# Bilinear block of a four-block fp32 network: the whole stacked image made by identity matmuls, in pieces between the convolution chunks, with no transfers

## Chip, cores and metric

The program runs on one core of one Trainium2 chip. The metric is the device time of one execution in microseconds; the times shown are medians of several executions. TensorE (PE; PEld is its weight load), VectorE (DVE), ScalarE (ACT), GpSimd (POOL) and SyncE (SP) run side by side and meet at semaphores. SBUF is the on-chip memory of 128 partitions, PSUM holds what TensorE writes, in eight banks (`ps[0]` to `ps[7]`) of 512 fp32 columns.

## The reference

Four residual blocks, each on the group-normalised image; x has 4 images of 32 channels of 64x64 pixels, in fp32. The change is in the second one.

```python
x = x + _L0_conv_ref(_gn(x), ...)   # dynamic convolution of 3x3 taps
x = x + _L1_conv_ref(_gn(x), L1_conv_weights, L1_conv_tap_offsets)   # the bilinear block
x = x + _L2_conv_ref(_gn(x), ...)   # four gated experts of two convolutions
x = x + _L3_conv_ref(_gn(x), ...)   # mixed weights, two convolutions
# _L1_conv_ref: nine taps with fractional offsets
ry = xp[:, :, y0i, :] * (1.0 - fy) + xp[:, :, y1i, :] * fy
tap = ry[:, :, :, x0i] * (1.0 - fx) + ry[:, :, :, x1i] * fx
out = jnp.einsum('kbiyx,oik->boyx', jnp.stack(taps, 0), weights)
```

With offsets from 0 to 3 every tap is a mix of pixels in a 4x4 window, so the block is one 4x4 convolution, whose weights (`WE`) are mixed once from the nine taps and their offsets.

## The kernel before

The image lies in SBUF with 32 partitions for each of the 4 images (4 x 32 = 128). `IMG` is the padded, normalised image, 68 rows of 66 columns. For the bilinear block `SK` holds, for each image b, a stack of four copies of it: partitions 32g to 32g+31 hold image b shifted by g columns (g = 0 to 3). With that stack four columns of the window times 32 channels make a contraction over all 128 partitions, and only the four rows of the window are left to loop over.

`conv(k, ...)` (L773 to L779) computes chunk k of the output, 8 rows or 512 pixels of all images. It has 16 matmuls: for each window row y (4) and each image b (4) one of 128x32 weights against 512 columns, the four images beside each other in the four column strips of the array, into bank `k % 4`. An fp32 matmul stands in the trace as two records, so a chunk has 32. There are `NCH` = 8 chunks, on L810. Chunk k reads the rows 8k to 8k+10 of `SK`.

`SK` is filled in two ways. The first 27 rows are made in pieces (`PIECES`, L80): `copy_piece(n)` (L781 to L791) sends one piece's rows of `IMG` through an identity matrix (`REPL`), 16 matmuls of 32x32, for each image b and each shift g, into the banks 4 to 7 (one for each image). The matmuls use all 16 sub-arrays of 32x32 side by side. VectorE then copies the banks of images 0 and 1 to `SK` (L1026 to L1030), ScalarE those of images 2 and 3 (L643 to L647). A piece cannot begin before both have copied the piece before it (L784 to L786), since it writes the same banks. Pieces 0, 1 and 2 stand ahead of chunk 0, piece 3 behind it. The other 40 rows, in three parts (`STACK_DMA`, L81), are moved by DMA: `copy_rows` (L321 to L327) issues 16 transfers for a part. SyncE issues parts 0 and 1 (L418 to L422), then the weights of the next block, `W2A` and `W2B` (L423 to L426). ScalarE issues part 2 after chunk 2 (L648 to L651). Chunks 3, 5 and 7 wait for a part each (L806, L807).

The instructions of an engine run in the order in which they stand in its block. On VectorE `add2(k)` (L1034 to L1040) adds the bank of chunk k to X and takes the statistics of the result, and `x2_done` tells that the bank is free for chunk k+4. After chunk 7 the statistics are joined (`coefs(3)`), VectorE writes `CP`, and the first convolution of the next block (L840) can begin; before it TensorE runs small matmuls of that block (L826, L827) and seven matmuls with an unused result, `fill(7)` (L832). An `If` that handles offsets beyond the window (`far`) is not taken with these inputs.

```python
for k in range(NCH):                      # L802
    if k < 3: wait stack1_by_vector, stack1_by_scalar >= k + 2
    if k in (3, 5, 7): wait stack1_by_dma[k // 2 - 1] >= 16 * 16
    if k >= 4: wait x2_done >= k - 3
    conv(k, lambda y: WE[:, y, :], 4, conv1_done)
    if k == 0: copy_piece(3)
```

(the waits are shortened here.)

Of the kernel before, what the change touches and what calls it, by code (L numbers as in the profile page):

```python
# [35 lines left out]
B, C, H, W = 4, 32, 64, 64  # L36
# [6 lines left out]
PW = W + 2  # L43
# [32 lines left out]
Z_IMAGE = Z_WEIGHT + 3  # L76
Z_LATER = Z_IMAGE + 3


PIECES = ((0, 8), (8, 11), (11, 19), (19, 27))  # L80
STACK_DMA = ((27, 43), (43, 59), (59, 67))  # L81
IMG_V = 40
RELU_ROWS = ((8, 16), (16, 24), (24, 32), (32, 40), (6, 8), (40, 48), (48, 56), (56, H - 1))
N_RELU = len(RELU_ROWS)
# [8 lines left out]
def build(nc, x, w0, pw, cw, w1, w2a, w2b, w3a, w3b, par, out):  # L93
    ctx = ExitStack()
    with ctx:
# [12 lines left out]
        def sem(name):  # L108
            return ctx.enter_context(nc.semaphore(name))
# [3 lines left out]
        IMG, img_at, _ = sb("IMG", [P, PH * PW])  # L113
# [58 lines left out]
        SK = SKF[:, :].rearrange("p (b n) -> p b n", b=B)  # L172
# [28 lines left out]
        zeroed = sem("zeroed")  # L201
# [30 lines left out]
        image_by_vector = sem("image_by_vector")  # L232
        image_by_scalar = sem("image_by_scalar")
        stack_copied = sem("stack_copied")
        stack1_by_vector = sem("stack1_by_vector")
        stack1_by_scalar = sem("stack1_by_scalar")
        stack1_by_dma = [sem(f"stack1_by_dma{i}") for i in range(len(STACK_DMA))]
        conv1_done = sem("conv1_done")
        x2_done = sem("x2_done")
        norm2_done = sem("norm2_done")  # L240
# [76 lines left out]

        def copied_piece(b, r0, r1):
            return ps[4 + b][:, 0:(r1 - r0) * W].rearrange("p (r c) -> p r c", c=W)

        def copy_rows(queue, part):  # L321

            r0, r1 = STACK_DMA[part]
            a, n = r0 * PW, (r1 - r0 - 1) * PW + W
            for b in range(B):
                for g in range(4):
                    queue.dma_start(SK[32 * g:32 * g + 32, b, a:a + n], IMG[32 * b:32 * b + 32, a + g:a + g + n]).then_inc(stack1_by_dma[part], 16)  # L327

        def relu_px(i):
            r0, r1 = RELU_ROWS[i]  # L330
# [9 lines left out]
        def _(sp):  # L340
# [74 lines left out]
            stack_third(2 * STEPS, 0, REST * P)  # L415
            repeat_hi(0, REST * P, STEPS + 1)

            sp.wait_ge(zeroed, Z_IMAGE)  # L418
            sp.wait_ge(image_by_scalar, 1)
            copy_rows(sp, 0)  # L420
            sp.wait_ge(image_by_vector, 2)
            copy_rows(sp, 1)  # L422
            for g in range(4):  # L423
                p = slice(32 * g, 32 * g + 32)
                sp.dma_start(W2A[p, :, :].rearrange("p (x d) n -> p x (d n)", x=3), w2a.rearrange("(x c) d n -> c x (d n)", x=3)).then_inc(w_l2, 16)
# [1 line left out]
            for n in range(NCH):  # L427
                k = 2 * (n % 4) + 1 - n // 4
# [7 lines left out]
        def _(gp):  # L436
            n = [0]
# [128 lines left out]
            far = gp.value_load(FARN[0:1, 0:1], min_val=0, max_val=1)  # L566
            with gp.If(far > 0):
                gp.wait_ge(far_over, 1)
            gp.wait_ge(stack1_by_vector, len(PIECES))
            for m in (CP[:, :], HP[:, :, :], HQ[:, :, :]):  # L570
                gp.memset(m, 0.0).then_inc(zeroed, 1)
            rstd(3)
# [31 lines left out]
        def _(act):  # L604
# [24 lines left out]
            for pair in range(2):  # L629
                g = STEPS * TIT + 2 * pair  # L630
                n = min(2, NT - g)
# [6 lines left out]
                                      bias=NMR[p, 0:1], scale=RS[p, 0:1])  # L638

            act.wait_ge(coef_ready, 1)  # L640
            for r0, r1 in ((26, 42), (10, 26)):
                norm(rows(IMG, 1 + r0, r1 - r0), r0, r1).then_inc(image_by_scalar, 1)
            for n, (r0, r1) in enumerate(PIECES):  # L643
                act.wait_ge(stack_copied, n + 1)
                for b in (2, 3):
                    ins = act.activation(stack_piece(b, r0, r1), copied_piece(b, r0, r1), ACT.Copy)
                ins.then_inc(stack1_by_scalar, 1)  # L647
            act.wait_ge(zeroed, Z_IMAGE)  # L648
            act.wait_ge(image_by_vector, 2)
            act.wait_ge(conv1_done, 3)  # L650
            copy_rows(act, 2)  # L651

            act.wait_ge(coef_ready, 2)
            act.wait_ge(zeroed, Z_LATER)
            act.activation(U[:, :], X[:, :], ACT.Identity, bias=NMR[:, 0:1], scale=RS[:, 0:1]).then_inc(norm2_done, 1)
# [41 lines left out]
        def _(pe):  # L697
# [83 lines left out]
            def copy_piece(n):  # L781

                r0, r1 = PIECES[n]
                if n:  # L784
                    pe.wait_ge(stack1_by_vector, n)
                    pe.wait_ge(stack1_by_scalar, n)  # L786
                for b in range(B):
                    p = slice(32 * b, 32 * b + 32)
                    for g in range(4):
                        ins = pe.matmul(ps[4 + b][32 * g:32 * g + 32, 0:(r1 - r0) * W], REPL[p, 0, :], image_piece(b, r0, r1, g), start=True, stop=True)  # L790
                ins.then_inc(stack_copied, 1)  # L791
# [5 lines left out]
            pe.wait_ge(image_by_vector, 1)  # L797
            copy_piece(0)
            copy_piece(1)
            pe.wait_ge(image_by_scalar, 2)  # L800
            copy_piece(2)
            for k in range(NCH):  # L802
                if k < 3:
                    pe.wait_ge(stack1_by_vector, k + 2)
                    pe.wait_ge(stack1_by_scalar, k + 2)
                if k in (3, 5, 7):  # L806
                    pe.wait_ge(stack1_by_dma[k // 2 - 1], 16 * 16)  # L807
                if k >= 4:
                    pe.wait_ge(x2_done, k - 3)
                conv(k, lambda y: WE[:, y, :], 4, conv1_done)  # L810
                if k == 0:
                    copy_piece(3)

            pe.wait_ge(far_known, 1)
            far = pe.value_load(FARN[0:1, 0:1], min_val=0, max_val=1)
# [104 lines left out]
        def _(ve):  # L920
            n = [0]
# [101 lines left out]
            coefs(2)  # L1023
            norm(rows(IMG, 1, 10), 0, 10).then_inc(image_by_vector, 1)
            norm(rows(IMG, 43, H - 42), 42, H).then_inc(image_by_vector, 1)
            for i, (r0, r1) in enumerate(PIECES):  # L1026
                ve.wait_ge(stack_copied, i + 1)
                for b in (0, 1):
                    ins = ve.tensor_copy(stack_piece(b, r0, r1), copied_piece(b, r0, r1))
                ins.then_inc(stack1_by_vector, 1)  # L1030

            ve.wait_ge(far_known, 1)
            far = ve.value_load(FARN[0:1, 0:1], min_val=0, max_val=1)
            def add2(k):  # L1034

                ve.wait_ge(conv1_done, k + 1)
                xs = X[:, k * CH:(k + 1) * CH]
                ve.tensor_tensor(xs, ps[k % 4][:, :], xs, ALU.add).then_inc(x2_done, 1)
                ve.wait_ge(x2_done, k + 1)
                return ve.bn_stats(ST[:, k, :], xs)  # L1040

            for k in range(NCH - 1):
                add2(k)
            ve.wait_ge(image_by_scalar, 2)
            with ve.If(far > 0):
                ve.wait_ge(mix_ready, 1)
# [204 lines left out]
```

## Time and profile before

| | |
|---|---|
| median of 3 runs | 425.21 us (425.14 to 425.44) |
| the profiled execution | 425.92 us, of which the span is 424.1 us |
| mean granted TensorE clock over the span | 0.966 of full speed |
| TensorE matmuls busy | 382.5 us, 90% |
| VectorE busy | 276.4 us, 65% |
| ScalarE busy | 57.3 us, 14% |
| transfers SK<-IMG of SyncE | 32, 131.8 KB each, 2.6 us to landing |
| bilinear block on TensorE | from 276.06 to 313.57 us |

The span is the time from the first to the last instruction in the profile; times within it are counted from its start. "Releaser" is what ended an engine's wait. The clock of TensorE is given as a share of its full speed: 1.00 is 2.4 GHz, 0.50 is 1.2 GHz. The chain of work that ended last follows, from the last instruction back, what each step waited for, so that the sum of its steps is the time.

### The profile page before, as it was taken

To read this page: it belongs to the slowest core of one execution; us is meant where nothing else is said; L and a number is where in the kernel's file an instruction comes from. 1 tells how busy PE (TensorE), PEld (TensorE's weight loads), DVE (VectorE), ACT (ScalarE), POOL (GpSimd) and SP (SyncE) were. 2 spreads that over 40 slices of the span, in tenths; PEclk is the share of its full clock that TensorE was granted. 3 is DMA by queue.
4 is the path that set the end of the run, shared out by engine and by line. 5 is a ranking of instruction groups with operands and counts; after the bars stand their busy time and mean duration, and the time that the engine had idled before them with its cause. 6 is when DMAs were issued, how large, how long until landed. Compare 5 with 4: busy or idle time off the path is not lost.

```text
span 424.1 us, 8245 instructions
## 1 busy us (share of the span) xinstructions
PE 382.5 (90%) x3174; PEld 259.1 (61%) x3174; DVE 276.4 (65%) x486; ACT 57.3 (14%) x95; POOL 91.1 (21%) x220
## 2 busy tenths in 40 slices
PE   0799799999999999999999999479999979889892
PEld 0344588888888888888888888312247652157570
DVE  4981377777877888887787798844444077831155
ACT  0721000000000000000000000041013027552200
POOL 6687500688800000000000000105000037000000
PEclk9999799999999999999999999859999999899997
DMA  6276758055455545535613400068900000000023
GB/s 204 61 182 153 186 142 220 7 144 130 120 123 125 146 104 139 151 86 143 162 49 96 109 2 0 1 152 195 218 19 2 3 2 0 2 2 5 3 79 123
DMA packets 19649, 40.17 MB, mean 95 GB/s; under 512 B 7328, under 2 KB 8224, under 8 KB 19040
## 3 DMA queue, kind: packets, MB, share of 16 engines
q1 hardware_dynamic: 18848, 38.63, 35.9%
q10 hardware_dynamic: 768, 1.08, 1.0%
q8 instruction: 23, 0.38, 0.4%
q14 instruction: 10, 0.08, 0.1%
HBM read 4.62 MB, written 2.10 MB: 16 GB/s over the span
## 4 chain that ended last, share of the span: by engine, by line
PE 75%; DVE 11%; SPq 5%; DMA 4%; issue 3%; ACT 2%; POOL 1%; DVEq 0%; POOLq 0%; ACTq 0%
PE ps L734 21%; PE ps L735 21%; PE ps L736 7%; PE ps L777 7%; PE ps L914 4%; PE ps L900 4%; PE ps L850 2%; DMA LS<-HS 2%; DMA X<-in_x 2%; PE ps L871 2%; SPq L379 2%; SPq L364 2%; PE ps L790 2%; DVE RED L974 1%; PE ps L840 1%
## 5 line engine op out<-in xcount | busy, mean ns | idle before, releaser
L734 PE MATMUL ps<-WA,HS 128*128 128x512 f32 x396 | 160.3, 405 | 1.7 <-DMA LS<-HS 1.7
L735 PE MATMUL ps<-WB,LS 128*128 128x512 f32 x396 | 157.6, 398 | 0.0
L992 DVE TENSOR_TENSOR PROD<-ps,PT 128x512 f32<-128x512 f32 x132 | 91.1, 690 | 46.2 <-PE ps L736 41.8
L974 DVE TENSOR_REDUCE RED<-PROD 128x32 f32<-128x512 f32 x132 | 89.1, 675 | 0.0
L734 PEld LDWEIGHTS ps<-WA,HS 128*128 128x128 f32 x396 | 75.5, 191 | 21.0 <-issue 1.8
L735 PEld LDWEIGHTS ps<-WB,LS 128*128 128x128 f32 x396 | 75.6, 191 | 16.5
L736 PE MATMUL ps<-WC,TS 96*128 96x512 f32 x132 | 52.7, 399 | 0.0
L628 ACT ACTIVATE P<-ps 128x256 f32 x15 | 5.8, 385 | 207.5 <-PE ps L749 207.5
L449 POOL MEMSET IMG<- 128x67 f32 x1 | 0.2, 154 | 155.5 <-DVE X L981 155.5
L777 PE MATMUL ps<-SK,WE 128*32 128x512 f32 x256 | 29.2, 616 | 0.0
L736 PEld LDWEIGHTS ps<-WC,TS 96*128 96x128 f32 x132 | 25.1, 190 | 5.9
L777 PEld LDWEIGHTS ps<-SK,WE 128*32 128x32 f32 x256 | 8.1, 113 | 21.8 <-issue 21.8
L704 PE MATMUL ps<-U,PWB 128*128 128x512 f32 x16 | 9.1, 718 | 13.3 <-DVE U L944 13.0
L714 PE MATMUL ps<-P,CWB 128*128 128x512 f32 x48 | 20.9, 594 | 0.0
L900 PE MATMUL ps<-IMG,W 32*32 32x512 f32 x576 | 18.9, 596 | 2.1 <-ACT IMG L637 2.1
L914 PE MATMUL ps<-HQ,W 32*32 32x512 f32 x576 | 18.9, 596 | 1.5 <-DVE HQ L1191 1.5
L832 PE MATMUL ps<-REPL,ONE 128*128 128x256 f32 x84 | 19.4, 385 | 0.3 <-DVE Q L1126 0.3
L832 PEld LDWEIGHTS ps<-REPL,ONE 128*128 128x128 f32 x84 | 15.6, 190 | 4.3 <-issue 2.0
L900 PEld LDWEIGHTS ps<-IMG,W 32*32 32x32 f32 x576 | 12.6, 103 | 7.9 <-issue 3.3
L914 PEld LDWEIGHTS ps<-HQ,W 32*32 32x32 f32 x576 | 12.6, 103 | 7.8 <-DVE HQ L1191 2.4
L714 PEld LDWEIGHTS ps<-P,CWB 128*128 128x128 f32 x48 | 9.0, 188 | 11.7 <-issue 11.7
L704 PEld LDWEIGHTS ps<-U,PWB 128*128 128x128 f32 x16 | 3.5, 232 | 18.0 <-issue 15.7
(189 smaller groups left out, 336.2 us busy)
## 6 DMA issues: line engine op xcount, KB each, us to landing
HS<-HI SPq DMA_DIRECT2D x72, 96.5 KB, 2.1
LS<-HS SPq DMA_DIRECT2D x6, 1158.0 KB, 6.8
TS<-LO SPq DMA_DIRECT2D x72, 80.0 KB, 2.1
SK<-IMG SPq DMA_DIRECT2D x32, 131.8 KB, 2.6
HS<-LO SPq DMA_DIRECT2D x24, 96.5 KB, 2.1
LS<-LO SPq DMA_DIRECT2D x24, 96.5 KB, 2.2
X<-in_x SPq DMA_DIRECT2D x4, 512.0 KB, 5.8
out_x<-OT SPq DMA_DIRECT2D x8, 256.0 KB, 2.0
```

The lines of the kernel that those rows point to most:

```text
L364: sp.dma_start(HS[half][32 * g:32 * g + 32, b, 0:m].bitcast(F32), HI[32 * b:32 * b + 32, bass.ds(s * SL + g, m)].bitcast(F32)).then_inc(st ...
L704: pe.matmul(pw_bank(k)[:, :], PWB[:, :, :, :], U[:, k * CH:(k + 1) * CH], start=True, stop=True).then_inc(pw_conv_done, 1)
L714: ins = pe.matmul(ps[4 + q % 2][:, :], CWB[:, i, :, :, :], P1[:, a:a + 16 * PW].rearrange("p (r h c) -> p r h c", h=2, c=PW)[:, :, 0, i % ...
L734: pe.matmul(ps[b][:, :], px(HS, dy * PW), WA[:, dy, :], start=(dy == 0), stop=False)
L735: pe.matmul(ps[b][:, :], px(LS, dy * PW), WB[:, dy, :], start=False, stop=False)
L736: pe.matmul(ps[b][:, :], px(TS, 0, 96), WC[:, :], start=False, stop=True).then_inc(tile_done, 1)
L777: ins = pe.matmul(ps[k % 4][32 * b:32 * b + 32, :], wt(y), rows(SK[:, b, :], k * CR + y, CR, 0), start=(y == 0), stop=(y == slots - 1))
L832: pe.matmul(ps[7][:, 0:2 * P], ONE[:, :], REPL[:, :, :].rearrange("p (a b) c -> p a (b c)", a=1).broadcast_to([P, 2, P]), start=True, stop ...
L900: ins = pe.matmul(ps[4 * h + b][32 * q:32 * q + 32, :], W3[p, 0, t, :], rows(IMG[p, :], QR * q + CR * h + t % 3, CR, t // 3), start=(t == ...
L914: ins = pe.matmul(ps[4 * n + q][32 * b:32 * b + 32, :], W3[p, 1, t, :], rows(HQ[p, b, :], CR * h + t % 3, CR, t // 3), start=(t == 0), sto ...
L974: ve.tensor_reduce(RED[j % 2][:, 32 * b:32 * b + 32], PROD[b % 2][:, :].rearrange("p (o e) -> p o e", e=E0), AX.X, ALU.add).then_inc(sum_d ...
L992: ve.tensor_tensor(PROD[b % 2][:, :].rearrange("p (o e) -> p o e", e=E0), ps[b][:, :].rearrange("p (o e) -> p o e", e=E0), para.rearrange( ...
```

## The change

- `PIECES` covers all 67 rows: (0, 8), (8, 11), and seven pieces of 8 rows from 11 on, nine in all instead of four. `STACK_DMA`, `copy_rows`, its 48 transfers and its semaphores are gone.
- On TensorE pieces 3 to 8 stand behind the chunks 0 to 5, one each. Each chunk waits for the copies of the pieces it reads (`k + 2` of them), and the piece behind chunk 1 waits for the rest of `IMG`.
- VectorE copies its share of pieces 0 to 3 as before, and the share of piece k+4 right behind `add2(k)`. ScalarE copies all nine in a row.
- ScalarE normalises the rows 10 to 26 ahead of 26 to 42 (before, the other way round), and TensorE waits for the first of them alone ahead of piece 2.
- SyncE issues the weights of the next block as soon as VectorE has copied two pieces. GpSimd's clearing of later buffers waits for four pieces, as before.

```diff
-PIECES = ((0, 8), (8, 11), (11, 19), (19, 27))
-STACK_DMA = ((27, 43), (43, 59), (59, 67))
+PIECES = ((0, 8), (8, 11)) + tuple((r, r + 8) for r in range(11, 67, 8))
...
-        def copy_rows(queue, part):
-            r0, r1 = STACK_DMA[part]
-            a, n = r0 * PW, (r1 - r0 - 1) * PW + W
-            for b in range(B):
-                for g in range(4):
-                    queue.dma_start(SK[32 * g:32 * g + 32, b, a:a + n], IMG[32 * b:32 * b + 32, a + g:a + g + n]).then_inc(stack1_by_dma[part], 16)
...
-            sp.wait_ge(zeroed, Z_IMAGE)
-            sp.wait_ge(image_by_scalar, 1)
-            copy_rows(sp, 0)
-            sp.wait_ge(image_by_vector, 2)
-            copy_rows(sp, 1)
+            sp.wait_ge(stack1_by_vector, 2)
...
-            gp.wait_ge(stack1_by_vector, len(PIECES))
+            gp.wait_ge(stack1_by_vector, 4)
...
-            for r0, r1 in ((26, 42), (10, 26)):
+            for r0, r1 in ((10, 26), (26, 42)):
...
-            act.wait_ge(zeroed, Z_IMAGE)
-            act.wait_ge(image_by_vector, 2)
-            act.wait_ge(conv1_done, 3)
-            copy_rows(act, 2)
...
-            pe.wait_ge(image_by_scalar, 2)
+            pe.wait_ge(image_by_scalar, 1)
             copy_piece(2)
             for k in range(NCH):
-                if k < 3:
-                    pe.wait_ge(stack1_by_vector, k + 2)
-                    pe.wait_ge(stack1_by_scalar, k + 2)
-                if k in (3, 5, 7):
-                    pe.wait_ge(stack1_by_dma[k // 2 - 1], 16 * 16)
+                pe.wait_ge(stack1_by_vector, k + 2)
+                pe.wait_ge(stack1_by_scalar, k + 2)
                 if k >= 4:
                     pe.wait_ge(x2_done, k - 3)
                 conv(k, lambda y: WE[:, y, :], 4, conv1_done)
-                if k == 0:
-                    copy_piece(3)
+                if k == 1:
+                    pe.wait_ge(image_by_scalar, 2)
+                    pe.wait_ge(image_by_vector, 2)
+                if k + 3 < len(PIECES):
+                    copy_piece(k + 3)
...
             for k in range(NCH - 1):
                 add2(k)
+                if k + 4 < len(PIECES):
+                    stack_share(k + 4)
```

On TensorE, from chunk 1 to the end of chunk 4 before (L777 is a convolution matmul, L790 one of a piece; the x15 rows are the rest of a chunk or a piece):

```order
L777 MATMUL ps<-SK,WE 32x512 [waits stack1_by_scalar,stack1_by_vector]
L777 MATMUL ps<-SK,WE 32x512 x15
L777 MATMUL ps<-SK,WE 32x512 [waits stack1_by_scalar,stack1_by_vector]
L777 MATMUL ps<-SK,WE 32x512 x15
L777 MATMUL ps<-SK,WE 32x512 [waits stack1_by_dma0]
L777 MATMUL ps<-SK,WE 32x512 x15
L777 MATMUL ps<-SK,WE 32x512 [waits x2_done]
L777 MATMUL ps<-SK,WE 32x512 x15
```

The same place now, from chunk 1 to chunk 3 (L758 is the convolution, L771 the piece):

```order
L758 MATMUL ps<-SK,WE 32x512 [waits stack1_by_scalar,stack1_by_vector]
L758 MATMUL ps<-SK,WE 32x512 x15
L771 MATMUL ps<-IMG,REPL 32x512 [waits stack1_by_vector,stack1_by_scalar,image_by_vector,image_by_scalar]
L771 MATMUL ps<-IMG,REPL 32x512 x15
L758 MATMUL ps<-SK,WE 32x512 [waits stack1_by_scalar,stack1_by_vector]
L758 MATMUL ps<-SK,WE 32x512 x15
L771 MATMUL ps<-IMG,REPL 32x512 [waits stack1_by_scalar,stack1_by_vector]
L771 MATMUL ps<-IMG,REPL 32x512 x15
L758 MATMUL ps<-SK,WE 32x512 [waits stack1_by_scalar,stack1_by_vector]
L758 MATMUL ps<-SK,WE 32x512 x15
```

A piece of 16 matmuls has moved in behind each of the chunks 1 to 5; behind chunk 0 there was one already.

On VectorE, the adds and statistics of chunks 0 to 2 before (L1038 the add, L1040 the statistics), behind the last two copies of piece 3 (L1029):

```order
L1038 TENSOR_TENSOR X<-ps,X 128x512 [waits conv1_done]
L1040 BN_STATS ST<-X 128x6 [waits x2_done]
L1038 TENSOR_TENSOR X<-ps,X 128x512 [waits conv1_done]
L1040 BN_STATS ST<-X 128x6 [waits x2_done]
L1038 TENSOR_TENSOR X<-ps,X 128x512 [waits conv1_done]
L1040 BN_STATS ST<-X 128x6 [waits x2_done]
```

The same place now, for chunks 0 to 2 (L1024, L1026), with the copies on L1012:

```order
L1024 TENSOR_TENSOR X<-ps,X 128x512 [waits conv1_done]
L1026 BN_STATS ST<-X 128x6 [waits x2_done]
L1012 COPY SK<-ps 128x8x64 [waits stack_copied]
L1012 COPY SK<-ps 128x8x64
L1024 TENSOR_TENSOR X<-ps,X 128x512 [waits conv1_done]
L1026 BN_STATS ST<-X 128x6 [waits x2_done]
L1012 COPY SK<-ps 128x8x64 [waits stack_copied]
L1012 COPY SK<-ps 128x8x64
L1024 TENSOR_TENSOR X<-ps,X 128x512 [waits conv1_done]
L1026 BN_STATS ST<-X 128x6 [waits x2_done]
```

Two copies of a piece have moved in behind the statistics of each of the chunks 0 to 4; the add of chunk 1 now stands behind the copies of the piece that runs behind chunk 1.

## Rows read from the trace of the kernel before

**Rows 1.** Chain that ended last: start us, duration us, engine, output tile, line.

```profile
279.59 1.11 PE ps L790 x32
280.72 0.63 DVE SK L1029 x2
281.44 2.02 PE ps L790 x32
283.46 4.89 PE ps L777 x32
288.35 1.10 PE ps L790 x32
289.45 24.20 PE ps L777 x222
313.64 0.53 PE ps L826 x6
```

**Rows 2.** Timeline, TensorE's weight loads: start us, duration us, engine, line, operation, tiles.

```profile
287.32 0.12 PEld L777 LDWEIGHTS ps<-SK,WE 128*32 128x32 f32 x4 [0.31 <-issue]
288.28 0.26 PEld L790 LDWEIGHTS ps<-IMG,REPL 32*32 32x32 f32 x32 [0.84 <-issue]
289.38 0.16 PEld L777 LDWEIGHTS ps<-SK,WE 128*32 128x32 f32 x8 [0.84 <-issue]
289.84 0.13 PEld L777 LDWEIGHTS ps<-SK,WE 128*32 128x32 f32 x4 [0.31 <-issue]
290.28 0.13 PEld L777 LDWEIGHTS ps<-SK,WE 128*32 128x32 f32 x4 [0.30 <-issue]
...
312.60 0.13 PEld L777 LDWEIGHTS ps<-SK,WE 128*32 128x32 f32 x4 [0.30 <-issue]
313.57 0.31 PEld L826 LDWEIGHTS ps<-W3E,REPL 32*128 32x128 f32 x6 [0.84 <-issue]
```

**Rows 3.** Busy time by stretch: PE, PEld, DVE, ACT, POOL, clock, DMA share, GB/s.

```profile
298.00:303.00 5.00, 5.00 (x52) 1.49 (x48) 1.39 (x2) 0.00 (x0) 0.00 (x0) 1.00 1.03 234
308.00:314.00 6.00, 6.00 (x62) 1.75 (x52) 1.94 (x4) 0.00 (x0) 0.00 (x0) 1.00 0.09 22
```

**Rows 4.** Timeline, queues of SyncE and ScalarE: the removed transfers, then SyncE's next one.

```profile
276.74 22.05 SPq L327 DMA_DIRECT2D SK<-IMG  x32
296.61 11.51 ACTq L327 DMA_DIRECT2D SK<-IMG  x16
298.83 0.59 SPq L425 DMA_DIRECT2D W2A<-in_w2a  x1
```

**Rows 5.** Timeline, VectorE's and ScalarE's copies of a piece, with VectorE's first adds.

```profile
289.61 1.08 ACT L646 ACTIVATE SK<-ps 128x512 f32<-128x512 f32 x2 [4.89 <-PE ps L790]
289.61 1.29 DVE L1029 COPY SK<-ps 128x512 f32<-128x512 f32 x2 [4.69 <-PE ps L790]
290.81 0.68 DVE L1038 TENSOR_TENSOR X<-ps,X 128x512 f32<-128x512 f32 x1
291.53 0.69 DVE L1040 BATCH_NORM_STATS2 ST<-X 128x6 f32<-128x512 f32 x1
...
296.54 0.69 DVE L1038 TENSOR_TENSOR X<-ps,X 128x512 f32<-128x512 f32 x1 [2.01 <-PE ps L777]
```

**Rows 6.** Timeline: piece 1 after its wait; ScalarE's next work; the next block's convolution.

```profile
279.59 0.96 PE L790 MATMUL ps<-IMG,REPL 32*32 32x192 f32 x32 [1.51 <-DVE SK L1029]
...
316.59 3.80 ACT L655 ACTIVATE U<-X,NMR,RS 128x4096 f32<-128x4096 f32 x1 [25.90 <-DVE NMR L933]
317.54 5.13 PE L840 MATMUL ps<-CP,W2A 32*128 32x320 f32 x72
```

**Rows 7.** Timeline, TensorE in the third block, where its clock falls once.

```profile
356.78 1.06 PE L886 MATMUL ps<-RE,REPL 128*32 128x512 f32 x8
364.62 1.93 PE L886 MATMUL ps<-RE,REPL 128*32 128x512 f32 x8
366.48 1.77 PE L871 MATMUL ps<-U,REPL 32*128 32x448 f32 x8
```

**Rows 8.** Busy time by stretch of the same place, columns as in rows 3.

```profile
366.00:367.00 1.00, 1.00 (x8) 0.52 (x8) 0.38 (x1) 0.00 (x0) 0.00 (x0) 0.50 0.00 0
```

More of the change, by code:

```diff
@@ L236, in build @@
         stack1_by_scalar = sem("stack1_by_scalar")
-        stack1_by_dma = [sem(f"stack1_by_dma{i}") for i in range(len(STACK_DMA))]
         conv1_done = sem("conv1_done")
@@ L1025, in _, with stack_share @@
             norm(rows(IMG, 43, H - 42), 42, H).then_inc(image_by_vector, 1)
-            for i, (r0, r1) in enumerate(PIECES):
+            def stack_share(i):
+                r0, r1 = PIECES[i]
                 ve.wait_ge(stack_copied, i + 1)
@@ L1030, in _ @@
                 ins.then_inc(stack1_by_vector, 1)
+            for i in range(4):
+                stack_share(i)
             ve.wait_ge(far_known, 1)
```

## The prediction

> **What bounds the kernel now.** I read the chain that ended last first, since only what stands on it costs time. In the bilinear block the chain is TensorE almost alone: chunk 0, then piece 3, then the other seven chunks as one step of 24.20 us, then the next block's first matmul [rows 1]. No transfer stands in it, though chunks 3, 5 and 7 wait for some. So the second question was whether these waits cost anything hidden in that step. The weight loads of TensorE answer it: a chunk has eight groups of loads, and they come at an even pace. From 290.28 (the fourth group of chunk 1) to 312.60 (the last of chunk 7) there are 52 steps in 22.32 us, 0.429 us each, so a chunk takes 8 x 0.429 = 3.43 us [rows 2], and none of the rows between them departs from that by more than 0.01 us. Third, the stretches: while the DMA engines were full (share 1.03) and when they were nearly idle (0.09), TensorE was busy throughout and its clock was 1.00 both times [rows 3]. The transfers neither hold TensorE up nor slow it. The block is bound by TensorE's own work.
>
> **What is removed.** 48 transfers: 32 on SyncE, which took its queue 22.05 us to issue, 16 on ScalarE in 11.51 us [rows 4]. ScalarE has nothing else to do there until 316.59, and SyncE's next work is the next block's weights, issued from 298.83 on; their first reader starts at 317.54 [rows 4, 6]. Nothing waits for these queues, so the removal gives back 0. The weights now go out some 17 us earlier (after piece 1, copied at 281.35 [rows 1]), which nobody needs: 0. The swapped order of ScalarE's two normalisations and the shorter wait ahead of piece 2: piece 2 starts at 281.44, right behind VectorE's copies of piece 1, which it waits for in both kernels [rows 1]. So it was not held by the image, and this gives 0 as well.
>
> **What is added on TensorE.** Five pieces, behind chunks 1 to 5. The trace has one of the same kind at full clock, piece 3 behind chunk 0, with the same tiles and neighbours. The cost is what the piece inserts into the even pace. The last load group of chunk 0 is at 287.32, the third of chunk 1 at 289.84 (the first two go together at 289.38): 2.52 us [rows 2]. Without a piece the third group comes three steps after that, 3 x 0.429 = 1.29 us. A piece costs 2.52 - 1.29 = 1.23 us. Its parts: 0.96 us from the last convolution load to the piece's first instead of 0.43, so 0.53 us until the array is free for the other form, then 1.10 us for the piece up to the next chunk's load, less 0.40 us because that chunk gets two groups at once [rows 2]. Bounds: from below the two passes of 512 columns alone, 2 x 0.43 = 0.86 us, from above 1.10 + 0.53 = 1.63 us, if nothing is won back. I take 1.23, the same event measured. 5 x 1.23 = **6.15 us**, with 4.3 and 8.2 as ends. All of it stands on the chain.
>
> The Trainium skill (TensorE: Matmul & The Clock Gate, Part 3, "Measured speedup vs the span model") gives a packed group of 16 tiles the duration of one matmul plus 15 x 4 ns. With the two passes as that duration this would be an estimated 0.92 us for each piece, 4.6 us in all and 429.8 us. It leaves out the change of tile form on both sides, which the row shows, so I don't take it.
>
> **The waits that it adds.** A piece writes the banks that VectorE and ScalarE must have emptied of the piece before. Both copy at once: the copies begin 0.16 us after the piece's last column (289.61 against 289.45) and take 1.29 us on VectorE and 1.08 us on ScalarE [rows 1, 5]. The period of a chunk with a piece is 3.43 + 1.23 = 4.66 us. Let a chunk end at T. Its piece ends at about T + 1.2, the copies at T + 2.7, and the next piece may start at T + 4.66: 2.0 us of slack. The next chunk reads only up to the piece before that, so its wait is met earlier still. On VectorE the add of a chunk and its statistics take 1.41 us (290.81 to 292.22) [rows 5], and the copies of a piece are queued ahead of the add of the chunk in front of it. So add and statistics end at T + 4.1, half a microsecond ahead of the next chunk's end and over a microsecond ahead of the next piece's. VectorE has 2.70 us of work in 4.66 us. Chunk k+4 waits for the add of chunk k, three periods back. Behind chunk 5 stands the last piece; its copies and the add of chunk 5 end at T + 4.1, chunk 6 ends at T + 4.66, so the adds of chunks 6 and 7 come as promptly as before, when VectorE waited 2.01 us for each chunk [rows 5]. All added waits: 0. GpSimd's clearing waits for four pieces, whose times don't move. ScalarE copies 1.08 us in each period: hidden.
>
> **The sum.** Everything behind chunk 7 hangs on it in the same order and moves by 6.15 us. The profiled execution took 425.92 us, 1.8 us more than its span of 424.1: 424.1 + 6.15 = 430.3 us of span, 432.1 us of execution. It lies 0.7 us above the median of the runs, 425.21, on which I base the forecast: 425.21 + 6.15 = **431.4 us**.
>
> **The rivals.**
>
> *The clock of the third block falls elsewhere.* Around 366 us the clock is at 0.50 (1.2 GHz), after a stretch in which TensorE had waited in between [rows 7, 8]. The two groups of matmuls there take 1.93 and 1.77 us, where the same eight of 512 columns take 1.06 at full clock [rows 7] and the eight of 448 about 0.95 by their columns. Both stand on the chain: (1.93 - 1.06) + (1.77 - 0.95) = 1.7 us. All this work moves by 6 us, and whether the fall comes again, not at all or twice can't be read from one trace. Without it 429.7 us, with a second one 433.1. For it: TensorE's pauses there are short, so it is near the edge. Against: the three runs of before lie within 0.3 us, so the fall is no matter of chance within one kernel.
>
> *The copies become the bound.* If each new piece were held until the one before is copied with nothing in between, TensorE would wait as ahead of piece 1, 1.51 us [rows 6]: 5 x 1.51 = 7.6 us more, 439.0 us. It decides only from the point where the copies are later by the slack of 2.0 us; with 2.70 of 4.66 us used I give it little. The Trainium skill (TensorEngine Tiling (Array Packing), "PSUM Bottleneck") says that tiling speeds up TensorE but not the emptying of PSUM, which may become the bottleneck. By that rule it would come out so; no row here shows it once a chunk lies between two pieces.
>
> *Not slower: the pieces slip in beside the convolution.* The array would have to run a piece's 32x32 tiles while the chunk's 128x32 tiles still stream, and load the next chunk's weights meanwhile. The kernel is not measurably slower if a piece costs less than 0.85 / 5 = 0.17 us. Then 425.2 to 426.0 us. Against it stands the one instance, which costs 1.23 us, with its first load held 0.53 us longer than the pace [rows 2].
>
> *The change does not do what it says*, for example because the removed transfers had hidden something: the order of the built instructions shows the six pieces and no transfer, so this has no chance of its own.
>
> **How the numbers follow.** Forecast (pieces at 1.23 us, same clock) 0.68: 431.4, from 430.8 to 432.0. Clock falls less: 0.13, 429.7. Clock falls more: 0.11, 433.1. Copies as the bound, in whole or in part: 0.05. Pieces cheaper or hidden: 0.03, of which 0.02 not slower. The range takes in both clock cases and, from below, the piece at its lower bound (429.5): 429.4 to 433.5. 0.2% of 425.2 us is 0.85 us, about what a measurement of this kernel tells from no change. Slower by more 0.97, within it 0.02, faster 0.01.
>
> **What would show it.** Six groups of piece loads, with 2.52 us between the last load group ahead of each and the third group behind it; the pace of 0.43 us inside chunks unchanged; TensorE with no idle time from piece 2 to the fill matmuls; chunk 7 ending at 319.8 instead of 313.6; VectorE's idle time ahead of its adds small for chunks 1 to 5 and near 2 us for 7 only. Wrong would be: idle time of TensorE ahead of a piece, released by VectorE or ScalarE; a piece that costs less than 0.9 or more than 1.6 us; a clock below 1.00 between 288 and 320 us; or a tail behind chunk 7 that is not the same length as before.

## The result, and the profile after it

Four executions of the changed kernel took 429.79 to 434.56 us, median 432.41, beside a median of 425.32 us for four of the kernel before. The ratio is 1.0194, with a 95% interval from 1.0133 to 1.0254. Slower was right; whether by more or by less than 2% the interval leaves open. The median lies 1.0 us above the forecast of 431.4 and inside the stated range of 429.4 to 433.5. The ratio applied to 425.32 gives 433.6 us, just outside it. (The plain ratio of the two medians is 1.0167.) Executions more than 1.5% above the fastest of the same kernel are called slow and don't enter a ratio; none of the four is one.

The bilinear block itself did what the sum says. The chain that ended last, of the changed kernel (start us, duration us, what), in the block:

```profile
281.89 4.77 PE ps L758 x32
286.66 1.10 PE ps L771 x32
287.76 3.59 PE ps L758 x32
291.35 1.08 PE ps L771 x32
292.43 3.60 PE ps L758 x29
296.03 1.09 PE ps L771 x32
...
311.22 7.04 PE ps L758 x64
318.26 0.53 PE ps L807 x6
```

It is TensorE alone, as in [rows 1]; the step of 24.20 us is now broken up by the pieces, and no wait stands between them. Its weight loads, around the first added piece (L771) and at the block's end:

```profile
290.30 0.14 PEld L758 LDWEIGHTS ps<-SK,WE 128*32 128x32 f32 x4 [0.29 <-issue]
291.28 0.24 PEld L771 LDWEIGHTS ps<-IMG,REPL 32*32 32x32 f32 x32 [0.84 <-issue]
292.36 0.17 PEld L758 LDWEIGHTS ps<-SK,WE 128*32 128x32 f32 x8 [0.84 <-issue]
292.82 0.14 PEld L758 LDWEIGHTS ps<-SK,WE 128*32 128x32 f32 x4 [0.29 <-issue]
...
318.19 0.31 PEld L807 LDWEIGHTS ps<-W3E,REPL 32*128 32x128 f32 x6 [0.84 <-issue]
```

From the last group ahead of the piece to the third behind it 2.52 us pass, the forecast number and the one of [rows 2]. From the piece behind chunk 0 to the next block's first load it was 313.57 - 288.28 = 25.29 us before, and is 318.19 - 286.59 = 31.60 us now (31.53 in the profiles of e1 and e13): **6.31 us more, 1.26 for each piece** (forecast 1.23).

The span grew by 8.6 us all the same, from 424.12 to 432.76. Its parts, each between the same two instructions of both kernels: up to the block's first weight load 276.02 before, 274.46 now, -1.56 us (that part of the program is the same in both, and it varies by as much between the profiles of other runs: 272.7 to 276.0); the block 37.55 and 43.73, +6.18 (0.12 of the 6.31 came back because chunk 0 took 4.77 us instead of 4.89); from the block's end to the end of the span 110.55 and 114.57, **+4.02**. The last term stood in the sum as nothing. Busy time by stretch, of the changed kernel (length; PE, PEld, DVE, ACT, POOL busy; granted clock; DMA share; GB/s):

```profile
349.00:353.00 4.00, 3.75 (x11) 3.04 (x11) 2.82 (x13) 1.02 (x2) 2.00 (x3) 0.57 0.00 0
369.00:373.00 4.00, 4.00 (x20) 0.78 (x18) 2.31 (x4) 1.26 (x2) 0.00 (x0) 0.58 0.00 0
380.00:383.00 3.00, 1.28 (x47) 0.72 (x60) 1.39 (x1) 2.89 (x2) 0.00 (x0) 1.00 0.00 0
383.00:387.00 4.00, 4.00 (x92) 2.58 (x82) 0.00 (x0) 2.40 (x1) 0.00 (x0) 0.57 0.01 4
404.00:407.00 3.00, 3.00 (x64) 0.98 (x40) 0.43 (x2) 0.55 (x2) 0.00 (x0) 0.50 0.02 5
```

The clock falls to 0.50 four times between the block and the end of the last convolution; in the profile of the kernel before it fell there once [rows 8]. (Behind the last convolution it is low in both.) The first two of the four are in the third block, the second of them near the fall of [rows 7]. The other two come at most 1.6 us after the start of the fourth block's two convolutions, each of which has a pause of TensorE ahead of it, and make both longer:

```profile
L881 PE MATMUL ps<-IMG,W 32*32 32x512 f32 x576 | 20.5, 643 | 2.2 <-ACT IMG L623 2.2
L895 PE MATMUL ps<-HQ,W 32*32 32x512 f32 x576 | 20.5, 642 | 1.5 <-DVE HQ L1179 1.5
```

(busy us, mean ns of one, then the idle time ahead and what ended it.) Before, they took 18.9 us each. That is 3.3 of the 4.0 us; the rest is the fall at 349, where 16 fill matmuls took 5.32 us instead of 3.72, partly under a wait for ScalarE.

### The profile page after: what moved, and what is told of

It is laid out like the page before. It is cut to its first block, busy times and chain, and to the rows that moved or that the text cites. A ratio compares the mean times of both kernels' runs of the same rounds, so it can differ in the third digit from the quotient of the medians.

```text
span 432.8 us, 8544 instructions
## 1 busy us (share of the span) xinstructions
PE 393.0 (91%) x3334; PEld 264.8 (61%) x3334; DVE 282.5 (65%) x496; ACT 62.9 (15%) x105; POOL 91.4 (21%) x220
## 4 chain that ended last, share of the span: by engine, by line
PE 77%; DVE 11%; SPq 5%; DMA 3%; issue 3%; ACT 1%; POOL 1%; DVEq 0%; POOLq 0%
PE ps L715 20%; PE ps L716 20%; PE ps L758 7%; PE ps L717 7%; PE ps L895 5%; PE ps L881 5%; PE ps L771 3%; PE ps L831 2%; PE ps L813 2%; DMA LS<-HS 2%; DMA X<-in_x 2%; SPq L369 2%; SPq L354 2%; DVE RED L955 1%; PE ps L852 1%
## 5 line engine op out<-in xcount | busy, mean ns | idle before, releaser
L758 PE MATMUL ps<-SK,WE 128*32 128x512 f32 x256 | 30.3, 617 | 0.0
L1012 DVE COPY SK<-ps 128x512 f32<-128x512 f32 (+1 forms) x18 | 10.9, 650 | 19.8 <-PE ps L771 19.8
L881 PE MATMUL ps<-IMG,W 32*32 32x512 f32 x576 | 20.5, 643 | 2.2 <-ACT IMG L623 2.2
L895 PE MATMUL ps<-HQ,W 32*32 32x512 f32 x576 | 20.5, 642 | 1.5 <-DVE HQ L1179 1.5
L758 PEld LDWEIGHTS ps<-SK,WE 128*32 128x32 f32 x256 | 8.1, 112 | 22.5 <-issue 22.5
L813 PE MATMUL ps<-REPL,ONE 128*128 128x256 f32 x84 | 21.0, 408 | 0.3 <-DVE Q L1114 0.3
L813 PEld LDWEIGHTS ps<-REPL,ONE 128*128 128x128 f32 x84 | 16.7, 205 | 4.7 <-issue 2.0
L881 PEld LDWEIGHTS ps<-IMG,W 32*32 32x32 f32 x576 | 14.9, 107 | 7.4 <-issue 3.9
L895 PEld LDWEIGHTS ps<-HQ,W 32*32 32x32 f32 x576 | 13.6, 107 | 8.4 <-DVE HQ L1179 2.4
L771 PE MATMUL ps<-IMG,REPL 32*32 32x512 f32 (+1 forms) x288 | 12.0, 692 | 6.3 <-DVE IMG L1001 3.9
```

What stands on the lines that cost most here:

```text
L758: ins = pe.matmul(ps[k % 4][32 * b:32 * b + 32, :], wt(y), rows(SK[:, b, :], k * CR + y, CR, 0), start=(y == 0), stop=(y == slots - 1))
L813: pe.matmul(ps[7][:, 0:2 * P], ONE[:, :], REPL[:, :, :].rearrange("p (a b) c -> p a (b c)", a=1).broadcast_to([P, 2, P]), start=True, stop ...
L881: ins = pe.matmul(ps[4 * h + b][32 * q:32 * q + 32, :], W3[p, 0, t, :], rows(IMG[p, :], QR * q + CR * h + t % 3, CR, t // 3), start=(t == ...
L895: ins = pe.matmul(ps[4 * n + q][32 * b:32 * b + 32, :], W3[p, 1, t, :], rows(HQ[p, b, :], CR * h + t % 3, CR, t // 3), start=(t == 0), sto ...
```

## The experiments

**How the executions are compared.** The single executions of one kernel turned out to spread over several us, so all executions are counted below and none is left out. (Eight of the 74 of before and one of e8 lie more than 1.5% above the fastest of their kernel. Without them the mean of before is 424.22, so that every other kernel stands 0.4 us higher against it, and that of e8 is 425.26.) Each execution has its span and its mean clock; (1 - clock) x 2 x span is the time that TensorE's clock was at 1.2 GHz. "+-" is one standard error. The mean of the kernel before is over the 74 executions that ran beside the experiments.

| kernel | executions | mean us | lowest to highest | mean us at 1.2 GHz |
|---|---|---|---|---|
| before | 74 | 424.62 +- 0.26 | 420.93 to 428.59 | 24.3 |
| changed (first, e1, e13) | 16 | 431.78 +- 0.38 | 428.24 to 434.56 | 28.5 |
| e2 before, delayed in the block | 6 | 433.34 +- 1.01 | 430.27 to 436.03 | 27.8 |
| e3 one matmul a piece | 6 | 430.56 +- 0.59 | 428.29 to 432.72 | 26.7 |
| e4 changed, pauses filled | 6 | 430.77 +- 0.64 | 428.43 to 432.70 | 25.6 |
| e5 one 128x32 matmul a piece | 2 | 428.16 +- 0.60 | 427.56 to 428.77 | 23.9 |
| e6 pieces twice | 2 | 436.36 +- 1.27 | 435.09 to 437.63 | 25.2 |
| e7 before, no transfers | 4 | 434.64 +- 1.09 | 432.15 to 437.31 | 39.0 |
| e8 before, early banks | 12 | 425.89 +- 0.78 | 423.78 to 432.81 | 28.4 |
| e9 before, pauses filled | 12 | 423.59 +- 0.47 | 420.80 to 426.24 | 22.0 |
| e10 early banks, pauses filled | 12 | 424.27 +- 0.44 | 421.89 to 427.51 | 26.3 |
| e11 before, 4 more fills | 12 | 427.27 +- 0.48 | 424.39 to 429.68 | 28.4 |
| e12 before, 8 more fills | 6 | 429.47 +- 1.01 | 425.93 to 431.43 | 27.5 |
| e14 before, 13 more fills | 6 | 431.31 +- 0.64 | 429.45 to 433.53 | 29.6 |
| e15 before, 2 more fills | 12 | 425.39 +- 0.27 | 423.91 to 426.82 | 24.2 |

Over the 74 executions of before, a straight line fitted to time against time at 1.2 GHz rises by 0.35 us for each us, with a correlation of 0.97.

The profiles show where such falls lie and what they cost. From the next block's first convolution (317.54 before) to the end of the span the work is the same in all 17 profiles, but for a few fill matmuls in pauses in e4, e9 and e10:

| profiles | falls in the third block | at the fourth block's convolutions | us to the end |
|---|---|---|---|
| e2, e5, e9, e12, e15 | 0 | 0 | 105.6 to 105.7 |
| before, e4 | 1 | 0 | 106.6, 106.7 |
| e3, e6, e8, e10, e14 | 2 | 0 | 107.2 to 107.3 |
| e11 | 1 | 1 | 108.0 |
| e1 (changed), e7 | 2 | 1 | 108.9 |
| e13 (changed) | 1 | 2 | 110.0 |
| changed, first | 2 | 2 | 110.6 |

The time behind the block follows from the number and the place of the falls, whichever kernel it is: with none, it is the same with pieces (e5), with plain fills (e12, e15) and with pads (e2). One or two falls in the third block cost 1.0 or 1.6 us in all, one at a convolution some 1.7 us more. That is the +4.02 of the first profile: one fall more in the third block and two at the convolutions. What the table leaves open is why the three profiles of the changed kernel have three or four falls each, and the others none to three.

**The changed kernel again (e1).**

> The changed kernel once more, in five rounds beside the kernel before. Theory A (the block costs 6.2 us, the rest of the difference is how often TensorE's clock falls in the third and fourth block, which differs between executions): the times spread over several us, between about 429.5 (no fall more than before) and 434.5 (three more, 1.3 to 1.7 us each); mean clock falls as the time rises, about 0.015 for 4.8 us. Theory B (the fall is a fixed effect of the change): all executions within 0.5 us of each other near 434.5.

Measured: 431.64 to 432.70 us, ratio 1.0185 (1.0137 to 1.0233), while the kernel before on the same chip spread from 421.11 to 428.59. Neither theory hit whole: the mean clock is 0.962 to 0.966 in all six. The changed kernel's six lay close together, though below 434.5, and the spread that I expected of it was found in the kernel before: with the same work, 15 to 36 us of its span are at 1.2 GHz. The three runs of 425.14 to 425.44 on which the forecast stood were three of a distribution 7.7 us wide.

**The kernel before, delayed (e2).** The pieces' time replaced by matmuls with an unused result, all transfers kept:

```diff
                 if k == 0:
                     copy_piece(3)
+                pad([0, 0, 0, 3, 3, 3, 2, 2][k])   # 128x256 matmuls into ps[7]
```

> The kernel before, with all its transfers, and 13 matmuls with an unused result (128x256, 0.46 us each by the fill rows) behind the chunks 3 to 7, so that all that follows the block comes 6.0 us later, about as in the changed kernel. Theory A: the same spread as the changed kernel, 429.5 to 434.5, median near 432, since only the shift matters; the removal of the transfers gives nothing. Theory B (the pieces or the missing transfers upset the later blocks): 425.2 + 6.0 = 431.2 in nearly every execution, with one fall in the third block as before. Theory C (the transfers cost something beside TensorE's matmuls): the mean lies above the changed kernel's.

The pads cost more than planned: 32.61 us from the piece behind chunk 0 to the block's end, 7.32 more than before, where 13 of 0.46 us make 6.0. Their tiles are 128x128 and not the convolution's, and the surplus of 1.3 us is 0.27 us for each of the five groups (an estimate), what a change of tile form costs in e3 below. The mean rose by 8.7 +- 1.0, so 1.4 +- 1.0 beyond the delay, and the executions reach from 430.27 to 436.03, wider than theory A had them and not the single value of theory B. The mean is 1.6 +- 1.1 us above the changed kernel's, of which the longer delay makes 1.0; what is left gives theory C no support.

**The price of a piece (e3, e5, e6).** All three are the changed kernel with pieces 4 to 8 altered. In e3 each has one 32x32 matmul, in e5 one matmul in the convolution's form, in e6 all 16 twice.

```diff
 def copy_piece(n):
-    for b in range(B): ... for g in range(4): matmul(...)      # 16 of 32x32
+    for b in range(B if n < 4 else 1): ... for g in range(4 if n < 4 else 1):   # e3
+    if n > 3: matmul(ps[4][0:32, ...], REPL[:, 0, :], rows(IMG, r0, r1 - r0, 0))   # e5: 128x32
+    for b in [b for _ in range(2 if n > 3 else 1) for b in range(B)]: ...   # e6
```

> The changed kernel, with one matmul of 32x32 in each of the pieces 4 to 8 instead of 16 (15 of the 16 parts of these rows of the stack are left out, the copies out of PSUM stay). If the price of a piece is its change of tile form and its two passes of 512 columns, with the 16 tiles side by side, a piece still costs at least 1.1 us and the kernel 430.5 to 431 us plus the falls of the clock. If the price is in the number of matmuls, a piece costs under 0.5 us and the kernel takes 427.5 or less.

> The changed kernel, with each of the pieces 4 to 8 replaced by one matmul in the convolution's own tile form, 128x32 over 512 columns (what lands in the stack's rows 27 to 66 is not the stack; the copies stay). Against the run with one 32x32 matmul in a piece only the tile form differs. If the change of form costs what the load rows say (0.53 us ahead of the piece beyond the pace, and more behind it), the time from the last load of a chunk to the third of the next falls from about 2.4 us to 2.1 us or less (1.29 of the pace and at most 0.86 of the two passes): a piece costs 0.86 us or less. If the form is not the point it stays at about 2.4 us.

> The changed kernel, with the 16 matmuls of each of the pieces 4 to 8 issued twice in a row. If a piece is 0.86 us of streaming and the rest is its two changes of form, the second copy adds 0.86 us each, 4.3 us in the block. If the whole price of 1.23 us belongs to the 16 matmuls, it adds 6.2 us.

The period of a chunk with its piece is read from the chain. Of e3 (L771 the piece, L758 the chunk):

```profile
290.86 0.97 PE ps L771 x2
291.83 3.58 PE ps L758 x31
295.41 0.97 PE ps L771 x2
```

Of e5 (L769 the one matmul of the piece, two records):

```profile
292.90 0.38 PE ps L769
293.28 3.43 PE ps L758 x29
...
297.19 0.38 PE ps L769
297.57 3.43 PE ps L758 x28
```

Of e6:

```profile
289.33 2.28 PE ps L771 x62
291.61 3.58 PE ps L758 x30
295.19 2.28 PE ps L771 x62
```

Without a piece the period is 3.43 us. It is 4.29 in e5 (293.28 to 297.57), 4.57 on average in e3 (290.86 to 295.41 is 4.55, the next 4.59), 4.69 in the changed kernel, 5.87 in e6. So the two passes of 512 columns cost 0.86 us even as a single matmul; the change of tile form adds 0.28; the other 15 matmuls add 0.12 together. A piece of one 32x32 matmul costs 1.14 us, within what I had expected (at least 1.1), and one without a change of form 0.86, at the bound that I had given it. That held. But the second copy of a piece, which changes no form, costs 1.18 us, where I expected 0.86 if the rest was the change of form, and 1.23 if the price belongs to the 16 matmuls. The second fits better, though e3 shows that fewer matmuls are hardly cheaper. The weight loads of e6 show something else between two groups of the same 16 tiles:

```profile
289.26 0.25 PEld L771 LDWEIGHTS ps<-IMG,REPL 32*32 32x32 f32 x32 [0.84 <-issue]
289.72 0.10 PEld L771 LDWEIGHTS ps<-IMG,REPL 32*32 32x32 f32 x1 [0.20 <-issue]
290.15 0.55 PEld L771 LDWEIGHTS ps<-IMG,REPL 32*32 32x32 f32 x31 [0.33 <-issue]
```

The first 32 loads go out in 0.25 us, the second 32 wait and then take 0.55. Why, these runs don't tell. By this price, joining two pieces behind one chunk would save under 0.1 us (no run did it).

**No transfers (e7).** The kernel before without them; GpSimd clears those rows of the stack instead.

```diff
-            copy_rows(sp, 0) ... copy_rows(sp, 1) ... copy_rows(act, 2)
+            gp.memset(SK[:, :, 27 * PW:67 * PW], 0.0).then_inc(rest_cleared, 1)
```

> The kernel before without the 48 transfers: rows 27 to 66 of the stack are zeros, written by GpSimd meanwhile, and not the image. If the transfers cost TensorE nothing, the block is as long as before (37.5 us) and the chunks keep the pace of 3.43 us. If they slowed it through SBUF, the chunks 1 to 7 get shorter. The change would have won that back.

In the chain, chunk 0, the piece and the other seven chunks:

```profile
290.25 5.04 PE ps L775 x32
295.30 1.10 PE ps L788 x32
296.40 24.21 PE ps L775 x215
```

The seven chunks take 24.21 us, with the transfers 24.20 [rows 1]. They cost TensorE nothing, so there was nothing to win back. The kernel's own time, 434.6 us, is another matter: the block began at 282.82 instead of 276.02, because this experiment's clearing held up VectorE (timeline, GpSimd and VectorE):

```profile
273.45 8.90 POOL L563 MEMSET SK<- 128x10560 f32 x1
273.50 10.12 DVE L1018 TENSOR_SCALAR IMG<-X,MV,RS 128x640 f32<-128x640 f32 x2
```

**Pauses and free banks (e4, e8, e9, e10).** Two edits: fill matmuls in the pauses ahead of and between the fourth block's convolutions (e4 on the changed kernel, e9 on the kernel before), and piece 1 in banks 0 to 3, which are idle there (e8, on the kernel before). e10 has both, on the kernel before.

```diff
-            fill(7)
+            fill(11)
...
+            pe.wait_ge(hidden3_by_vector, 2)
+            pe.wait_ge(hidden3_by_scalar, 2)
+            pad(3, 0)                       # into ps[0], free by then
             pe.wait_ge(hidden3_by_vector, 4)
...
-            return ps[4 + b][...]
+            return ps[(0 if r0 == 8 else 4) + b][...]
-                if n: wait stack1_by_vector, stack1_by_scalar >= n
+                if n > 1: wait for n if n > 2 else 1
```

> The changed kernel, with four more matmuls of unused result ahead of the fourth block's first convolution and three between its two convolutions, into pauses of 2.2 and 1.5 us. Theory A with pauses as the trigger: the falls at 383 and 404 us (within the two convolutions) are gone, so the executions lie between 429.5 and 432 us with a mean clock of 0.966 or more. Rival (the fall there does not come from the pause ahead of it): the spread up to 434.5 stays.

> The kernel before, with piece 1 written to banks 0 to 3, which are free there, so that it need not wait for the copies of piece 0, and piece 2 waits for the copies of piece 0 alone. If the pauses of 1.51 and 0.90 us ahead of pieces 1 and 2 are the cost they seem to be, the block gets 1.5 to 2.0 us shorter (35.6 to 36.0 us instead of 37.5) and the mean of the executions 1.5 to 2 us lower. If something else is late next (the copies, the normalised image), it gets under 0.8 us.

> The kernel before with the pauses ahead of and between the fourth block's convolutions filled, as in the filled variant of the changed kernel. Theory A (pauses are followed by falls there in some executions): the mean of the executions is 0.5 to 1.5 us below that of the kernel before (424.7 so far) and none lies above 427. Rival (the falls there are no matter of the pauses): the same mean and spread, 421 to 428.6.

> Piece 1 in the free banks and the pauses of the fourth block filled, on the kernel before. The block is 1.3 us shorter (measured), and if the falls ahead of the fourth block's convolutions are what took that back, the mean is 422 to 423.5 us, below both kernels. If the falls elsewhere (third block) took it back, 424 to 425.

In the profile of e4 the clock is 1.00 at the start of both convolutions, after the filled pauses:

```profile
383.00:387.00 4.00, 4.00 (x146) 2.87 (x134) 0.00 (x0) 0.86 (x1) 0.00 (x0) 1.00 0.01 4
403.00:407.00 4.00, 4.00 (x138) 2.67 (x113) 0.00 (x0) 0.00 (x0) 0.00 (x0) 1.00 0.01 4
```

That single profile proves little: the clock is full at both convolutions in 9 of the 14 profiles of kernels without this filling too (table above), and in all three with it.

The means fell by 1.0 +- 0.7 (e4 against changed), 1.0 +- 0.5 (e9 against before) and 1.6 +- 0.9 us (e10 against e8). None alone is clear of noise. e9 fell as theory A says, none above 427. e4 reached from 428.4 to 432.7, beyond what I had given it on both sides, with mean clocks down to 0.963. Weighted together it is 1.1 +- 0.4 us, and 0.8 +- 0.4 without the executions more than 1.5% above the fastest. That points to a gain from the filling and doesn't prove one; that it costs nothing is shown (105.65 us to the end in e9, as without it).

e8 shortened the block by 1.3 us (274.76 to 310.98 is 36.2, before 37.55), less than the 1.5 expected at least. The pauses gave 1.8 us (chunk 0 begins 5.60 us after the first piece on the chain, before 7.40), but chunk 0, now earlier against the clock's rise at 284.0, took 5.35 us instead of 4.89. In the mean nothing of that was seen: 1.3 +- 0.8 us above before, with 4 us more at 1.2 GHz. e10 came to 424.27, 0.3 +- 0.5 us below before: not the 422 to 423.5 that I expected, but the rival's 424 to 425, and its profile has two falls in the third block and none in the fourth. No version beats the kernel before by more than its noise: the ratio of e9 is 0.9995 (0.9955 to 1.0035), of e10 1.0021 (0.9983 to 1.0058).

**Is it the pieces, or being later? (e11 to e15).** Longer `fill(7)` behind the block, in the kernel before, with 4, 8, 13 and 2 more, and the changed kernel once more:

```diff
-            fill(7)
+            fill(7 + n)
             pe.wait_ge(w_l2, 128)
```

> The kernel before with four more matmuls of unused result (1.84 us) behind the bilinear block, all else the same. If the later blocks' falls of the clock are chance alone, the mean is 424.7 + 1.8 = 426.5, within 0.6 us. If it matters by how much the later work is moved, the mean leaves that by more, in either direction.

> The same with eight more (3.68 us). Chance alone: 428.4 within 0.6 us. If the amount of the move matters: off that line, and by another amount than with four.

> The changed kernel again, beside e14 on the same chip. Chance alone: mean of the executions at 424.5 + 6.2 = 430.7, and the first ten at 432.3 were bad luck. Position or pieces: 431.8 or more.

> The kernel before with 13 more matmuls of unused result (6.0 us) behind the bilinear block. If the later blocks have more falls because they come later, the mean is 431.5 or more (1 us over 424.5 + 6.0) and the time at half clock near that of the changed kernel. If the pieces cause them, 430.5 within 0.5 us.

> The kernel before with two more fills (0.92 us). Chance alone, or falls from the pieces: 425.4 within 0.5 us. If every move away from the place that the kernel before has costs falls: 426 or more.

From the profiles (block's end to the next convolution, 3.97 us before) the work was moved by 1.73, 3.46 and 5.62 us in e11, e12 and e14, and 0.87 in e15. The means rose by more than that: 0.9 +- 0.6, 1.4 +- 1.0 and 1.1 +- 0.7 us beyond the move; with e2, 1.1 +- 0.4 together. In e15 nothing was beyond it (-0.1 +- 0.4), and with it the five together are 0.4 +- 0.3. So e11 and e12 lie above the 0.6 us that I had given to chance alone, e15 within its 0.5; e14's 431.31 lies between its two cases (431.0 at most, 431.5 at least), with 29.6 us at 1.2 GHz near the changed kernel's 28.5. The changed kernel's excess over its 6.3 us is 7.16 - 6.31 = 0.9 +- 0.5. e13 alone had none: 430.90, 5.7 us above the kernel before of the same chip (425.22). Counted against the kernel before on the same chip, the excess is 1.2 to 1.9 us in e1, e2, e11 and e12 and -0.7 to 0.5 in e13, e14 and e15, which ran on another chip: it goes with the chip as much as with the edit. So no difference is seen between the pieces and plain fills of the same length in what they do to the later blocks, and whatever excess there is, is about 1 us. Whether it is real or the luck of these executions, sixteen of the changed kernel don't settle; the size of the move, as such, is not shown to matter.

## Why the prediction was right or wrong

**The bound.** Right. TensorE's own work bounds the block; the transfers were not on the chain, and without them the pace was the same (e7).

**What is removed gives 0.** Right: nothing came back, neither from the queues nor from the earlier weights or the swapped normalisation. Piece 2 again started right behind VectorE's copies (279.87, the copies done at 279.78). Nor do the 1.56 us that the first profile gained ahead of the block come from there: the low stretch near 50 us was half as long in it as before, and TensorE waited 1.1 us for `LS` instead of 1.7.

**A piece at 1.23 us, 6.15 in all.** Right: 1.26 and 6.31. Reading the price from the pace of the loads around the one existing piece was the right way, since the piece alone (1.10 on the chain) would have given 5.5. The parts that I gave it were half right. The two passes are 0.86 (e5), but the change of form is 0.28 and not 0.37 (e3 against e5), and a piece without any change of form still costs 1.18 (e6). The span model of the Trainium skill (TensorE: Matmul & The Clock Gate, Part 3) would have put a piece at an estimated 0.92 us. The trace has 1.26. The model's price for more tiles (15 x 4 ns, 0.06 us) is half of what e3 shows, 0.12 us for 15 matmuls; what it lacks most is the 0.28 us of the change of form.

**The added waits cost 0.** Right. From piece 2 on, VectorE waited for TensorE and never the other way round: from 281.9 to 320 us the view of waits has no row for TensorE (who waited, how long in all, how often, longest; changed kernel, 286 to 318 us):

```profile
DVE SK L1012 <- PE ps L771: 15.0, 6, 4.6
DVE X L1024 <- PE ps L758: 0.9, 1, 0.9
```

Ahead of copies it waited 2.07 us each time, and its add of chunk 1 stood behind the copies without holding up anyone, as the slack said. So the rival of the copies as the bound, and the Trainium skill's "PSUM Bottleneck" (TensorEngine Tiling (Array Packing)) with it, does not hold here: in each period of 4.69 us the copies of a piece took 1.29 us on VectorE and 1.09 on ScalarE.

**The base and the clock: the step that failed.** "The three runs of before lie within 0.3 us, so the fall is no matter of chance within one kernel." It is: 74 executions of the same kernel spread from 420.9 to 428.6, with 15 to 36 us at 1.2 GHz. The steps that failed are the sentence "Everything behind chunk 7 hangs on it in the same order and moves by 6.15 us", which puts the change of the work behind the block at nothing, and the rival that allowed one fall more or less, with 0.24 of the chance. In the first profile that work became 4.02 us longer, and the profiles have from none to four falls there. The mechanism of the rival held as far as the traces go: the four falls of the first profile each come within 2 us behind waits of TensorE of 0.6 to 2.2 us; that the waits cause them is argued and not shown. Its place was right in part, for it named the third block alone, and two of the three falls more are at the fourth block's convolutions. Its size was wrong both ways: a single fall in the third block lengthens the work to the end by 1.0 us (before and e4 against the five profiles without a fall), not by the 1.7 that I read by adding up two groups of matmuls; one at a convolution costs 1.7; and they come several at a time.

How much of this is luck: single executions scatter by 2.2 us (before) and 1.5 us (changed), one standard deviation, so the difference of two medians of four has a standard error of some 1.6 us (an estimate from these two). A range 4.1 us wide could easily be missed by it; twice that error to both sides is over 6 us. The forecast itself stands nearly as a statement on the mean: base 424.62, 0.6 below the one I used, plus 6.31 is 430.9, measured 431.8 +- 0.4. Whether the 0.9 +- 0.5 us between them is more than chance stays open.

**The not-slower rival.** Excluded by e3, e5 and e6: even one matmul of two passes costs 0.86 us in the pace.

## What to carry to other kernels

A transfer that is hidden costs nothing, and to replace it by work on the engine that bounds the stage costs all of that work: price it from the pace around one existing instance, not from the duration of the instance. Before a difference of one or two per cent is explained, look at how much of each execution TensorE's clock was low; one us at the low clock is worth about a third of a us here, and three close runs don't show the spread. Compare profiles with the same number of falls, stage by stage: stages that seemed to differ by up to 5 us then agreed to 0.1. Where TensorE pauses for one to two us ahead of a long run of matmuls, a few unused matmuls in the pause cost nothing here; that they pay was not clear of noise.

## What the runs showed of the hardware

- One kernel, same inputs: from 15 to 36 us of a span of about 423 us with TensorE at 1.2 GHz, from execution to execution, and 7.7 us between the fastest and the slowest. A pause of 2.1 us ahead of L900 was followed by full clock in the profile of before, one of 2.2 us ahead of L881 by a fall in that of the changed kernel. At the fourth block's first convolution the clock fell in 5 of the 14 profiles without fills in the pause.
- A fall at one of these convolutions lengthened it from 18.9 to 20.5 us. With no fall, the work from the third block's first convolution to the end took 105.60 to 105.65 us in five profiles of five kernels.
- A second group of 16 matmuls of 32x32 on the same tiles costs 1.18 us, nearly as much as the first with its two changes of tile form (1.26). Sixteen such matmuls cost only 0.12 us more than one.
- A clearing on GpSimd of 10560 columns (8.90 us) held a VectorE operation from SBUF to SBUF for its whole length: one of 9.2 us where the same takes 0.61 (e7). ScalarE's normalisation beside it took 2.38 us as always. The Trainium skill (SBUF — State Buffer, Terms) says that VectorE and GpSimd share a port pair held for a full instruction. This row agrees.
